# Adaptive-norm attention layer with a mixture of experts on one core: routing divided between engines, marks on VectorE, gathers and the first tile's preparation moved ahead

## What is computed

```python
h = layernorm(x) * (1 + ca) + sa                       # x: 2 x 2048 x 256, mods from silu(c) @ wmod
q, k, v = relu(h Wq' + bq), relu(h Wk' + bk), h Wv' + bv
s = gamma * s + k_t v_t' ;  z = gamma * z + k_t         # a scan over the sequence
x = x + ga * (q_t s) / (q_t . z + 1e-6)
h = layernorm(x) * (1 + cb) + sb
expert = argmax(h Wr' + br)                            # 8 experts, 256 -> 1024 -> 256
x = x + gb * (relu(h W1[expert]' + b1[expert]) W2[expert]' + b2[expert])
```

## Time and profile before

| | |
|---|---|
| median of 3 runs | 469.73 us |
| profiled execution | 469.46 us, span 467.6 us |
| mean granted TensorE clock | 0.968 of full speed |
| busy: TensorE, VectorE, ScalarE, POOL | 423.6, 376.8, 332.9, 291.5 us |
| attention part | to about 206 us |
| expert part | from about 217 us |

### The profile page before, as it was taken

The page is one execution under the profiler, slowest core; times in us unless marked ns, Lnnn a source line. Parts: engine busy times, 40 slices in busy tenths (PEclk is TensorE's granted clock), DMA queues, the critical chain, the costliest instruction groups (busy, mean ns, idle before and its releaser), DMA issues.

```text
span 467.6 us, 14514 instructions
## 1 busy us (share of the span) xinstructions
PE 423.6 (91%) x4698; PEld 384.3 (82%) x4698; DVE 376.8 (81%) x1021; ACT 332.9 (71%) x844; POOL 291.5 (62%) x467
## 2 busy tenths in 40 slices
PE   7999899999998998965697479999999999999993
PEld 4988788988897887844687379999999999999993
DVE  2978999999999999895599537878878787778863
ACT  1558889999988888853675437777777777777770
POOL 2033677677776779987759966665666665664332
PEclk9999999999999999997898769999999999999998
DMA  8625355555565454112410011321212222200000
GB/s 287 239 91 187 107 160 158 164 177 177 175 207 176 140 169 137 46 57 69 146 38 13 23 57 51 100 70 54 69 50 66 64 63 66 68 25 27 20 18 2
DMA packets 23448, 46.91 MB, mean 100 GB/s; under 512 B 4683, under 2 KB 17228, under 8 KB 21200
## 3 DMA queue, kind: packets, MB, share of 16 engines
q1 hardware_dynamic: 17424, 31.82, 20.9%
q0 software_dynamic: 4992, 12.60, 8.8%
q10 hardware_dynamic: 960, 1.57, 1.0%
HBM read 35.22 MB, written 13.50 MB: 104 GB/s over the span
## 4 chain that ended last, share of the span: by engine, by line
PE 44%; DVE 30%; POOL 12%; issue 8%; DMA 2%; ACT 2%; DVEq 1%; POOLq 1%; ACTq 0%
PE ps_o L1832 18%; PE ps_qk L1806 10%; PE ps_va L1806 10%; DVE w L1072 4%; POOL wqk_b L523 4%; DVE arena L1283 3%; DVE arena L1276 2%; POOL arena L523 2%; DVE st L1286 2%; DMA w<-in_wmod 2%; DVE arena L1312 2%; DVE arena L971 2%; DVE logits L1297 2%; DVE arena L1268 1%; DVE st L884 1%
## 5 line engine op out<-in xcount | busy, mean ns | idle before, releaser
L1832 PE MATMUL ps_o<-w,arena 128*128 x912 | 106.6, 273 | 0.0
L1832 PEld LDWEIGHTS ps_o<-w,arena 128*128 128x128 f16 x912 | 87.8, 98 | 10.3 <-issue 0.5
L810 ACT ACTIVATE arena<-ps_qk,arena 128x128 f32<-128x128 f32 x156 | 44.5, 368 | 61.5 <-PE ps_qk L1806 58.7
L1417 DVE COPY w<-w 128x2048 f16 x78 | 60.3, 775 | 32.8 <-PE ps_qk L1806 26.1
L660 POOL DMA_INDIRECT out_rows<-arena,slot_token x39 | 46.4, 1190 | 33.8 <-POOL arena L654 29.8
L1403 DVE TENSOR_TENSOR arena<-arena 128x512 f16<-128x512 f32 x78 | 55.0, 705 | 9.6 <-ACT arena L818 9.5
L1806 PE MATMUL ps_qk<-arena,w 128*128 128x128 f16 x936 | 61.8, 225 | 0.9 <-issue 0.9
L1806 PE MATMUL ps_va<-arena,w 128*128 128x128 f16 x936 | 60.6, 223 | 2.0 <-DVE w L1417 2.0
L1806 PEld LDWEIGHTS ps_qk<-arena,w 128*128 128x128 f16 x936 | 58.5, 101 | 2.8 <-issue 1.9
L1806 PEld LDWEIGHTS ps_va<-arena,w 128*128 128x128 f16 x936 | 57.2, 100 | 2.7 <-DVE w L1417 2.2
L654 POOL TENSOR_TENSOR arena<-arena 128x256 f32<-128x256 f32 x38 | 27.5, 723 | 48.8 <-DVE arena L1509 48.8
(11 more groups left out here) (268 smaller groups left out, 883.4 us busy)
## 6 DMA issues: line engine op xcount, KB each, us to landing
w<-in_w_raw SPq DMA_DIRECT2D x16, 1024.0 KB, 5.5
token_rows<-arena SPq DMA_DIRECT2D x64, 128.0 KB, 2.7
arena<-in_x SPq DMA_DIRECT2D x32, 128.0 KB, 2.2
b_sb<-in_b2b SPq DMA_DIRECT2D x1, 1024.0 KB, 5.7
w<-in_wmod ACTq DMA_DIRECT2D x1, 768.0 KB, 8.4
w<-in_wqkv SPq DMA_DIRECT2D x1, 768.0 KB, 8.1
arena<-token_rows,slot_token POOLq DMA_INDIRECT x39, 3.5
out_rows<-arena,slot_token POOLq DMA_INDIRECT x39, 2.6
```

The source lines that it names most:

```text
L810: last = act.activation(hid[:, f, :], bank[("qk", "va")[h]][:, (f % 4) * P:(f % 4 + 1) * P], ACT.Relu, bias=consts_now[:, r, f:f + 1], sca ...
L1417: dve.tensor_copy(now[:, :, i * F // 2:(i + 1) * F // 2], of[:, :, i * F // 2:(i + 1) * F // 2]).then_inc(s_w1, 1)
L1832: last = pe.matmul(bank[f"o{n % 2}"][:, 0:D], hid_parts[:, r % 2, b, f, :], w[:, bass.ds(m, 1), a, f * D:(f + 1) * D].rearrange("p a d -> ...
```

## The change

- The early routing begins a slot sooner (20) and is divided: POOL does four operations over 128 elements in slots 25 and 26 and the multiplication by the codes in slot 29 (`early_places`); VectorE keeps the rest, in another order.
- All marks that POOL made are VectorE's, four chunks in one instruction: early ones in slots 28 (one) and 29 (three), late ones two each behind the rows of tiles 2, 3 and 4. The comparison behind `s_hot` moves from tile 1's rows to tile 2's (`late_tiles`), `late_matrices` from tile 2's to tile 4's. ScalarE waits for `minus_slot` alone.
- TensorE's early number matmuls are in slot 30 in front of the transposes, VectorE's `early_tokens` in slot 31.
- Gathers 0 and 1 are at the end of POOL's slot 31, gather 2 at the end of slot 33 ahead of `tile_constants`, which takes the constants of tiles 0 to 3; gather 3 is behind the last inverse deviations, ahead of the norms.
- `first_tile`, with the last matrix's low part, is at the start of slot 33 of VectorE, ahead of the residual of chunk 31.
- TensorE has 8 filler matmuls in place of 4 behind the gate's rows, and 8 in place of 6 behind the first transposes.

The diff, cut to its core (of `early_route_1` to `_3` only new or moved lines):

```diff
@@ -150,7 +150,7 @@
-POOL_MARKS = 24
+DVE_MARKS = 24
@@ -380,7 +381,7 @@
-        slot_a, tile_a16 = before_a[:, 80:80 + NA], before_a[:, 96:96 + NA // 2].bitcast(F16)
+        slot_a, tile_a16 = (before_a[:, i:i + NA // 2].bitcast(F16) for i in (80, 96))
@@ -517,11 +524,21 @@
-            def mark_slots(of, numbers, i):
-                for n in range(i * MARKS, (i + 1) * MARKS):
-                    last = pool.tensor_scalar(of[:, n, :], slot_no16, numbers[:, n:n + 1], None, ALU.is_equal)
-                last.then_inc(s_bits, 1)
+            def early_places(s):
+                if s == NA + 9:
+                    pool.wait_ge(s_limit, 1)
+                    pool.tensor_tensor(of_experts(upto_a), of_experts(upto_a), chosen_a, ALU.mult).then_inc(s_early, 1)
+                    pool.tensor_tensor(of_experts(place_a), of_experts(place_a), by_expert(firstc_a, NA),
+                                       ALU.add).then_inc(s_early, 1)
+                if s == NA + 10:
+                    pool.wait_ge(s_early, 2)
+                    pool.tensor_tensor(place_a, place_a, upto_a, ALU.mult).then_inc(s_early, 1)
+                    pool.tensor_tensor(chosen_a, chosen_a, of_experts(upto_a), ALU.subtract).then_inc(s_removed, 1)
+                if s == NA + 13:
+                    pool.wait_ge(s_hot, 1)
+                    pool.tensor_tensor(in_tile_a, in_tile_a, code16[:, 0:NA].unsqueeze(2).to_broadcast([P, NA, TA]),
+                                       ALU.mult).then_inc(s_numbers, 1)
@@ -566,21 +593,21 @@
                 pool.wait_ge(s_routed, 1)
-                constants_of(0)
-                constants_of(1)
+                for n in range(4):
+                    constants_of(n)
...
                     inverse_deviations(j, s_mv2, mv2, rs2, s_rs2s, s_rs2)
+                    if k == NCH // B + 1:
+                        fourth_gather()
...
                     inverse_deviations(j, s_mv1, mv1, rs1, s_rs1s, s_rs1)
-                if 0 <= (i := 2 * k + u - (NCH - MARKS)) < MARKS:
-                    pool.wait_ge(s_minus, 1)
-                    mark_slots(in_slot_a, slot_a, i)
+                early_places(B * k + u)
@@ -601,16 +628,14 @@
+                if (k, u) == (NCH // B - 1, 1):
+                    first_gathers()
                 if (k, u) == (NCH // B, 1):
-                    first_gathers()
+                    third_gather()
...
-            pool.wait_ge(s_x1, NCH)
-            for n in range(2, 4):
-                gather(n)
-                constants_of(n)
@@ -637,15 +662,10 @@
                     constants_of(n)
-                if TA - 6 <= s < TA - 3:
-                    i = s - TA + 6
-                    if i == 0:
-                        pool.wait_ge(s_minus, 2)
-                        pool.wait_ge(s_hot, 2)
-                        pool.tensor_tensor(in_tile, in_tile, code16.unsqueeze(2).to_broadcast([P, NCH, TB]),
-                                           ALU.mult).then_inc(s_numbers, 1)
-                    mark_slots(in_slot, slot_f, 2 * i)
-                    mark_slots(in_slot, slot_f, 2 * i + 1)
+                if s == TA - 5:
+                    pool.wait_ge(s_hot, 2)
+                    pool.tensor_tensor(in_tile, in_tile, code16.unsqueeze(2).to_broadcast([P, NCH, TB]),
+                                       ALU.mult).then_inc(s_numbers, 1)
@@ -1117,90 +1137,86 @@
+            def mark_slots(of, numbers, i):
+                these = slice(i * MARKS, (i + 1) * MARKS)
+                dve.tensor_tensor(of[:, these, :], slot_no16.unsqueeze(1).to_broadcast([P, MARKS, P]),
+                                  numbers[:, these].unsqueeze(2).to_broadcast([P, MARKS, P]),
+                                  ALU.is_equal).then_inc(s_bits, 1)
...
+                    mark(dve.memset(within_a, 1.0))
...
+                    hop(dve.tensor_copy(count_a.bitcast(I32), upto_a[:, NA - 1:NE * NA:NA]))
...
+                    hop(dve.tensor_scalar(firstc_a, first_a, float(TA + 1), float(P), ALU.min, ALU.mult))
+                    mark(dve.tensor_tensor(take_a, endc_a, firstc_a, ALU.subtract))
...
+                    dve.wait_ge(s_early, 3)
+                    mark(dve.tensor_reduce(pos_a, place_a.rearrange("p (e n) -> p n e", e=NE), AX_X, ALU.add))
...
+                    mark(dve.tensor_copy(slot_a, slot_ai.bitcast(I32)))
+                    mark(dve.tensor_copy(tile_a16, tile_ai.bitcast(I32)))
...
+                    mark_slots(in_slot_a, slot_a, 1)
+                if s == NA + 14:
+                    mark(dve.tensor_reduce(tile_af, late_a, AX_X, ALU.add))
+                if s == NA + 15:
+                    early_tokens()
+            def early_route_2(s):
...
+                    mark(dve.memset(within_a[:, 0:NE * NA:NA], 0.0))
+                if s == NA + 7:
+                    hop(dve.tensor_copy(full_a, full_ai.bitcast(I32)))
+                    mark(dve.tensor_tensor_scan(end_a, con("ones")[:, 0:1].to_broadcast([P, NE]), full_a, 1.0,
+                                                ALU.mult, ALU.add))
+                if s == NA + 8:
+                    dve.tensor_tensor(of_experts(upto_a), by_expert(take_a, NA), of_experts(place_a),
+                                      ALU.is_gt).then_inc(s_limit, 1)
+                if s == NA + 11:
+                    mark(dve.tensor_copy(pos_ai.bitcast(I32), pos_a))
+                if s == NA + 12:
+                    dve.tensor_tensor(in_tile_a, tile_a16.unsqueeze(2).to_broadcast([P, NA, TA]),
+                                      tile_no16[:, 1:TA + 1].unsqueeze(1).to_broadcast([P, NA, TA]),
+                                      ALU.is_equal).then_inc(s_hot, 1)
+                if s == NA + 13:
+                    mark_slots(in_slot_a, slot_a, 2)
+                if s == NA + 14:
+                    mark(dve.tensor_scalar(tile_matrix[:, 0:TA], tile_af, 2.0, None, ALU.mult))
+            def early_route_3(s):
+                if s == NA + 4:
+                    mark(choose(8, NA, 0))
+                level()
+                if s == NA + 5:
+                    mark(choose(8, NA, 3))
...
+                    mark(dve.tensor_scalar(endc_a, end_a, float(TA + 1), float(P), ALU.min, ALU.mult))
+                    mark(dve.tensor_tensor(first_a, end_a, full_a, ALU.subtract))
...
+                    mark(dve.tensor_scalar(tile_ai.bitcast(I32), pos_ai.bitcast(I32), 7, None, ALU.arith_shift_right))
+                    mark(dve.tensor_scalar(slot_ai.bitcast(I32), pos_ai.bitcast(I32), P - 1, None, ALU.bitwise_and))
...
+                    mark_slots(in_slot_a, slot_a, 0)
+                if s == NA + 13:
+                    mark_slots(in_slot_a, slot_a, 3)
@@ -1243,8 +1259,11 @@
                     return
-                routing = NA + 5 <= B * k + u < NA + 14
+                routing = NA + 4 <= B * k + u < NA + 16
                 attend, score = att_item(k, u, ATTEND), att_item(k, u, SCORE)
+                if (k, u) == (FULL, 1):
+                    level()
+                    first_tile(matrix_number(0))
@@ -1298,8 +1317,6 @@
-                if (k, u) == (FULL, 0):
-                    early_tokens()
@@ -1368,8 +1384,11 @@
                 mark(dve.tensor_copy(tile_16, tile_i.bitcast(I32)))
-                dve.tensor_copy(slot_f, slot_i.bitcast(I32)).then_inc(s_minus, 1)
+                mark(dve.tensor_copy(slot_f, slot_i.bitcast(I32)))
+            def late_tiles():
@@ -1457,14 +1476,12 @@
-            def first_tile():
+            def first_tile(m):
...
                 dve.wait_ge(s_b2, 16)
-                level()
-                m = matrix_number(0)
@@ -1513,6 +1530,11 @@
                     if n == 2:
+                        late_tiles()
+                    if n in (2, 3, 4):
+                        for i in ((0, 1), (2, 3), (4, 5))[n - 2]:
+                            mark_slots(in_slot, slot_f, i)
+                    if n == 4:
@@ -1719,17 +1741,17 @@
                               start=True, stop=True).then_inc(s_rank, 1)
-                if (it := att_item(k, u, XPOSE)) and it[0] > 0:
-                    transpose_x(it[0], it[2])
-                if B * k + u == NCH - 1:
-                    pe.wait_ge(s_ht, NCH)
-                    pe.wait_ge(s_hot, 1)
+                if B * k + u == NCH - 2:
+                    pe.wait_ge(s_ht, NCH - 1)
+                    pe.wait_ge(s_numbers, 1)
...
                     last.then_inc(s_ids, 1)
+                if (it := att_item(k, u, XPOSE)) and it[0] > 0:
+                    transpose_x(it[0], it[2])
@@ -1742,22 +1764,23 @@
             rows_of_width(both("o0"), gate_bt).then_inc(s_gbrow, 1)
-            keep_busy("k", 4)
+            keep_busy("k", 8)
...
                 pe.wait_ge(s_chosen, 2)
+                pe.wait_ge(s_removed, 1)
...
-                pe.wait_ge(s_numbers, 1)
+                pe.wait_ge(s_numbers, 2)
```

80 lines of the change are left out of this document (25 added, 55 removed).

## The result

The changed kernel takes 462.6 us (median of 4 runs, 462.2 to 463.2) where the kernel before, measured beside it, takes 469.4 us: a ratio of 0.9861, with a 95% interval of 0.9839 to 0.9883. The gain is 6.8 us; I had forecast 14.7 and a range that ended at 461.0. In the profiled execution the span is 460.3 us, 7.3 less than before.

A forecast was written before the change was run, and what follows sets the result against it. Before 280 us, TensorE's waits for gathered tokens (11.8 us) and POOL's marks (9.8 us) bound it. Tile 7 14.7 us sooner, 5.6 of them at tile 1 (1.5 from attention), gave 454.8, forecast 455.0 us; range 450.5 to 461.

The forecast's parts named there:

- Late marks: Tiles 1 to 7: marks moved from POOL to VectorE, 0.62 us each, shorten this stretch from 53.2 to 44.1 us.
- the standstill: Slot 4 of the tiles: VectorE stands still beside POOL's multiplication by the codes, 1.4 us (0 to 2.1).
- +3.5 if each mark stands still: Tiles' marks on VectorE: forecast time 3.5 us longer if each mark stands still as the 2.51 us row did.
- The wait for the marks that stays: TensorE near 252 us: a wait of about 5 us for VectorE's marks stays in place of the 9.8 us.
- The rule of the Trainium skill that I set against the change: Tiles: a two-SBUF-input VectorE operation and a GpSimd one reading SBUF exclude one another; standstill up to 1.8 us.
- The doubled rate of two-input 16-bit operations: Marks on VectorE: two-input 16-bit operations run at twice the rate, a mark then costing about 0.4 us.
- Attention part: Attention slots 20 to 31: 1.5 us gained in slots 20 to 27, 0 in 28 to 31; chunk 30's residual at about 201.5.
- VectorE has 3.0 us free in slots 28 to 31, so the marks about fill what POOL frees: Attention slots 28 to 31: four early marks, 2.5 us, fit VectorE's free time; net 0, from 1 us gain to 1.5 loss.
- Front: Gathers, last matrix and first tile, ahead of tile 1: tile 1 at 221.3, 5.6 us sooner, 1.5 of them from attention.
- 3.2 us for 2.9 us: POOL's queue ahead of the last inverse deviations: gather 2 and two constants, 3.2 us, replace gathers 0 and 1, 2.9 us.
- The second rival: Ahead of tile 1: last norms or a token-waiting gather hold tile 1, only marks gain 9.1 us, 460.6 us; chance 0.16.
- Low clock: Tiles 1 to 6: VectorE-bound gaps keep TensorE's clock at 1.2 GHz, 23 us more, 478 us; rival's chance 0.04.

The follow-up runs named there:

- experiments 4 and 8: Changed kernel with the late codes' multiplication moved from POOL to VectorE (4), 461.3 us; changed kernel with tile marks ahead of VectorE's row work (8), 461.5 us.
- experiment 3: Changed kernel with early marks 1, 2 and 3 each issued a second time on VectorE: 464.1 us, ratio 0.9872.
- kernel 16: Changed kernel with gathers 0, 1 behind chunks 28 and 29's deviations, 2, 3 behind the last ones, constants 2, 3 behind norms, first tile behind last residual: 460.7 us.
- Kernel 9: Changed kernel with gathers 0 and 1 back at their old place in POOL's queue, behind the norms of chunks 28 and 29: 465.0 us, ratio 0.9883.
- kernel 5: Changed kernel with early marks 2 and 3 moved from slot 29 to slot 30 and the tokens one slot later: 464.1 us, ratio 0.9890.
- kernel 11: Kernel before with late marks on VectorE, gathers 0 and 1 behind chunks 28 and 29's deviations, gather 2 behind the last, gather 3 behind norms: 462.2 us.
- kernel 14: Kernel 11 with gather 3 moved right behind gather 2 in POOL's queue, ahead of the last two norms: 460.8 us, ratio 0.9828.
- 14 to 17: Kernel 14 (460.8 us); with codes on VectorE, marks first, numbers later (15, 456.5); with the change's early routing and marks (16, 460.7); with both (17, 457.0).
- Experiment 10: Changed kernel with only gather 0 and the first tile's constant ahead of the last inverse deviations, gathers 1 to 3 behind them: 463.7 us, ratio 0.9853.

## Why the prediction was wrong

**Late marks: right in kind, a term undersized.** From tile 1 to tile 7 I forecast 44.1 us and 46.75 came. VectorE's copies lie 6.73, 6.26, 6.95 and 7.86 us apart, forecast 6.4, 5.7, 6.4 and 6.8. The two last have the marks in them, 0.91 us each for 0.62, and the standstill, 2.0 us for the gate (2.47 - 0.47) for 1.4; experiments 4 and 8 show both parts. The two first, 0.9 us over in sum, have no marks in them: VectorE is idle for 0.42 and 0.52 us ahead of the copies there, and no run was made on it. I had the other end in the range ("+3.5 if each mark stands still"). The wait for the marks that stays, "about 5 us", was 4.6, tile 6 took 7.45 us for 7.79, and after tile 7 a tile took 5.53 us for 5.52, as forecast. The rule of the Trainium skill that I set against the change (SBUF — State Buffer, Who interferes with whom) holds in both places: with POOL's operation gone from beside it, the two-input operation on VectorE takes 0.47 and 0.64 us. The doubled rate of two-input 16-bit operations (VectorE: DVE Perf Modes, The perf-mode tier table) is not seen: 0.64 us for 512 elements is the rate of the 1.15 us row for 960, with nothing beside it. In both operations one input repeats a single value along the row; no run here has plain rows on both sides, so whether that keeps the rate down stays open.

**Attention part: a gain forecast, a loss measured.** The step was "VectorE has 3.0 us free in slots 28 to 31, so the marks about fill what POOL frees". The free time was real but in the wrong slot. It lies in slot 30, where VectorE waits for ScalarE (1.20 us in one piece), and three of the marks stand in slot 29: a mean over four slots hid that. The mark in slot 28 also took 1.21 us, beside two operations of POOL, where the other three took 0.68. The slots 20 to 27 gave no gain either (46.5 us for 46.15). The residual of chunk 30 was then 2.3 us late, 3.8 from the forecast. What that costs hangs on the order of POOL's queue. In the changed kernel's order a further shift of 1.66 us reached tile 1 in full (experiment 3, 1.87 us); in the order of kernel 16 a shift of 2.25 us did not arrive at all.

**Front: this is the step that failed.** I wrote "So the inverse deviations start where they did, less the 1.5 us of the attention part, and tile 1 at 222.6 - 1.5 + 0.2 = 221.3". That puts the last deviations at 215.3; they started at 219.35, and tile 1 came at 225.83. What I said of the queue between the two pairs of deviations, "3.2 us for 2.9 us", was right to 0.5 us (13.62 us before, 13.35 after). But all of it lay later than I had it, and the loss is there in full when POOL's norm of chunk 29 ends: at 213.20, where my sum has 210.23 - 1.5 = 208.7. Two things hold this norm, side by side. The first is what I left out: "the two gathers (2.94 us, 210.41 to 213.35) leave this place", but they went to just ahead of the deviations of chunks 28 and 29, in the same in-order queue, on the same chain. Those started 3.0 us later (206.00 for 203.00), and ScalarE waited 4.41 us for them. The second is the term of the attention part: its 1.5 us of gain came as a loss. Kernel 9 parts the two. With the gathers out of the way that norm still ends at 212.36, 2.1 us later than before, since ScalarE waits for VectorE's low part; the gathers' new place adds 0.84 us to that. Moving the gathers was still a net gain of 1.7 us at the last deviations (219.35 for 221.06 in kernel 9). It was not free, though, as I had counted it, and kernel 16 shows a place where they cost less: the norm ends at 211.83 there.

The second rival, "a gather queued ahead of the norms", came nearest and had 0.16 of the chance; only in kernel 5 did the gather wait for its tokens, as that rival has it, and in the changed kernel its own place was enough. It gave 460.6, and the undersized standstill makes up the rest (4.5 missing at tile 1 and 2.65 behind it are 7.2 of the 7.6 us between 455.0 and 462.6). The range ended at this rival, but with the marks at their middle size: I had not let the two go wrong together.

**Low clock: a small part.** It did not decide, but it takes back what is won: tile 6 starts in it (0.58 in 265 to 270 us), and with the late gather 3 it is why kernel 11's early tile 1 was worth little. From tile 1 to tile 2 that kernel took 10.42 us, for 7.04 in kernel 14: TensorE waited 1.93 us for tokens, and its granted clock was 0.55 in 223 to 226 us and 0.50, the lower level, in 230 to 232, where kernel 14 had 1.00; the hidden matmuls took 2.60 us for 1.50 and the rows 4.04 for 2.92.

**What stays open.** No run has the gathers' new place without the attention part's lateness, so how late the norm of chunk 29 would be by the gathers alone is not measured; the two overlap, and their shares add up only in the order given above. Moving the first tile ahead of the last residual was never taken out by itself: the kernels with it behind the residual (14 to 17) also have other gathers. Experiment 10 bounds it from one side: there POOL waits 0.93 us for the last statistics, so with a better queue it is the next thing in the way.
